# The fold of the attention projections on ScalarE in place of VectorE, and 32 batches in groups of 4, 3 and 1

## What is computed

```python
def _proj(x, W1, b1, W2, b2):
    h = jnp.einsum('bsd,od->bso', x, W1) + b1
    return jnp.einsum('bsd,od->bso', h, W2) + b2
...
qp = _proj(q, W1, b1, W2, b2); kp = _proj(k, W1, b1, W2, b2)
qk = jnp.einsum('bqd,bkd->bqk', qp, kp) * scale + mask
attn = jax.nn.softmax(qk, axis=-1)
return jnp.einsum('bqk,bkd->bqd', attn, v1)
...
x = x + jnp.tanh(g_xattn[0]) * xattn(_layernorm(x), ctx, ctx, mask, W1, b1, W2, b2)
x = x + jnp.tanh(g_ffn[0]) * ffn(_layernorm(x), w1, b1, w2, b2)
```

## Time and profile before

| | us |
|---|---|
| median of 3 runs | 66.02 (65.62 to 68.14) |
| profiled execution | 65.45 |
| its span | 63.7 |
| TensorE busy | 57.5 (90%) |
| VectorE busy | 55.9 (88%) |
| ScalarE busy | 49.5 (78%) |
| GpSimd busy | 43.4 (68%) |

### The profile page before, as it was taken

The page is one execution under the profiler, slowest core; times in us unless marked ns, Lnnn a source line. Parts: engine busy times, 40 slices in busy tenths (PEclk is TensorE's granted clock), DMA queues, the critical chain, the costliest instruction groups (busy, mean ns, idle before and its releaser), DMA issues.

```text
span 63.7 us, 1845 instructions
## 1 busy us (share of the span) xinstructions
PE 57.5 (90%) x541; PEld 44.9 (71%) x541; DVE 55.9 (88%) x313; ACT 49.5 (78%) x137; POOL 43.4 (68%) x88
## 2 busy tenths in 40 slices
PE   4999699899989999989999999999999989998820
PEld 4989447568768775879579699959798849465410
DVE  4659979999999999999999999988999898989630
ACT  2701365597999699999999999999999988867700
POOL 5957599969996805999982996798963948570000
PEclk9999999999999999999999999999999999999998
DMA  0899999999991000000030001330000413041232
GB/s 0 235 395 383 399 416 406 418 408 415 398 396 63 9 0 5 0 5 10 5 124 0 0 0 55 111 140 33 0 0 0 162 42 140 0 165 68 102 124 82
DMA packets 3324, 9.09 MB, mean 143 GB/s; under 512 B 369, under 2 KB 754, under 8 KB 3314
## 3 DMA queue, kind: packets, MB, share of 16 engines
q1 hardware_dynamic: 3312, 8.98, 36.7%
q10 hardware_dynamic: 2, 0.00, 0.0%
HBM read 6.88 MB, written 2.10 MB: 141 GB/s over the span
## 4 chain that ended last, share of the span: by engine, by line
PE 56%; DVE 21%; ACT 5%; DMA 5%; POOL 4%; issue 4%; ACTq 1%; DVEq 0%; POOLq 0%
PE bank_O L545 10%; PE bank_A L504 9%; PE bank_H L530 8%; PE bank_S L488 7%; PE bank_T L464 6%; DVE st L653 6%; PE bank_T L479 5%; DMA load_sb<-in_packed 5%; PE bank_A L497 4%; DVE sc L708 4%; DVE load_sb L720 3%; ACT h L636 3%; POOL rs L381 3%; PE bank_O L540 2%; DVE mv L656 2%
## 5 line engine op out<-in xcount | busy, mean ns | idle before, releaser
L636 ACT ACTIVATE h<-bank_H,fb_q 128x512 int8<-128x512 f32 (+2 forms) x29 | 17.7, 650 | 1.9 <-PE bank_H L530 1.9
L381 POOL TENSOR_TENSOR rs<-ve,half 128x3 f32<-128x3 f32 (+5 forms) x9 | 10.5, 1164 | 8.8 <-DVE nm L661 8.8
L653 DVE BATCH_NORM_STATS2 st<-load_sb 128x6 f32<-128x128 f32 x64 | 14.0, 277 | 1.2 <-DMA load_sb<-in_packed 1.1
L398 POOL TENSOR_SCALAR xq<-load_sb,nm,rs 128x128 int8<-128x128 f32 x28 | 12.4, 459 | 0.9 <-POOL rs L381 0.2
L609 ACT ACTIVATE pr<-sc,mn 128x120 f32<-128x120 f32 x32 | 12.3, 394 | 0.0
L388 POOL TENSOR_SCALAR xn<-load_sb,nm,rs 128x128 f32<-128x128 f32 x22 | 9.7, 451 | 0.5
L504 PE MATMUL bank_A<-load_sb,prT 120*128 120x128 f32 x64 | 9.2, 285 | 0.4 <-ACT prT L618 0.4
L545 PE MATMUL bank_O<-w_q,h 128*128 128x128 bf16 x128 | 9.3, 219 | 0.3
L720 DVE SCALAR_TENSOR_TENSOR load_sb<-bank_A,rec,load_sb 128x128 f32<-128x128 f32 x32 | 9.1, 343 | 0.4 <-issue 0.2
L504 PEld LDWEIGHTS bank_A<-load_sb,prT 120*128 120x128 f32 x64 | 7.8, 191 | 1.9 <-ACT prT L618 1.8
L488 PEld LDWEIGHTS bank_S<-kpT,xaT 128*128 128x128 f32 x64 | 8.1, 191 | 1.3 <-issue 0.8
(11 more groups left out here) (80 smaller groups left out, 96.0 us busy)
## 6 DMA issues: line engine op xcount, KB each, us to landing
load_sb<-in_packed SPq DMA_DIRECT2D x6, 496.0 KB, 8.0
out_y<-y_sb SPq DMA_DIRECT2D x6, 256.0 KB, 2.1
load_sb<-in_packed SPq DMA_DIRECT2D x2, 512.0 KB, 11.1
load_sb<-in_packed SPq DMA_DIRECT2D x1, 576.0 KB, 13.9
load_sb<-in_packed SPq DMA_DIRECT2D x1, 514.0 KB, 6.8
...
```

What stands on the lines that cost most here:

```text
L381: nc.gpsimd.tensor_tensor(rs[:, at], ve[:, at], half[:, 0:at.stop - at.start], ALU.pow).then_inc(rs2_done, 1)
L398: nc.gpsimd.tensor_scalar(low_byte(xq16[g % RING], tile(j)), x_of(g, j), nm2[:, of(g, j, 1)], rs[:, roots(2, g, j)], ALU.add, ALU.mult).th ...
L636: nc.scalar.activation(low_byte(h16[g % RING], hcols(c, g)), bank_H[c][:, cols(g)], ACT.Relu, bias=fb1_q[:, c:c + 1]).then_inc(h_act[c], 1)
L653: nc.vector.bn_stats(st[:, START[g] + j, :], x_of(g, j)).then_inc(st_done, 1)
```

## The change

The six steps of `fold_cp1` and `fold_cp2` are now ScalarE activations, with the same waits. Group 0 has four tiles where it had three, the last group one where it had two. One tile of normalising and one of quantising go from GpSimd to VectorE, and the tile that ScalarE normalises is of group 1 instead of group 0. `DUE` and `FILLERS` have new numbers throughout.

```diff
-TILES = [3, 4, 4, 4, 4, 4, 4, 3, 2]
+TILES = [4, 4, 4, 4, 4, 4, 4, 3, 1]
...
-XN_ON_POOL = [1, 2, 3, 2, 4, 3, 2, 3, 2]
-XN_ON_ACT = [1, 0, 0, 0, 0, 0, 0, 0, 0]
-XQ_ON_POOL = [1, 3, 4, 4, 4, 4, 4, 3, 1]
+XN_ON_POOL = [1, 2, 3, 2, 4, 3, 2, 3, 1]
+XN_ON_ACT = [0, 1, 0, 0, 0, 0, 0, 0, 0]
+XQ_ON_POOL = [1, 3, 3, 4, 4, 4, 4, 3, 1]
...
 DUE = dict(
-    stats1=[380, 574, 771, 1149, 1307, 1670, 2499, 3091, 3649],
+    stats1=[385, 517, 727, 1155, 1287, 1834, 2617, 3438, 4074],
...
-FILLERS = [9, 28, 2, 2, 5]
+FILLERS = [10, 22, 14]
...
+            def fold_cp1():
...
+                act.wait_ge(fold_mm, 1)
+                nc.scalar.activation(Wc[:, :], bank_H[1][:, 0:D], ACT.Identity, accum_out=Wc_sum[:, :]).then_inc(fold_cp, 1)
+                nc.scalar.activation(bc[:, :], bank_H[1][:, D:D + 1], ACT.Identity, bias=b2_sb).then_inc(fold_cp, 1)
+                act.wait_ge(fold_cp, 2)
+                nc.scalar.activation(lift[:, :], Wc_sum[:, :], ACT.Identity, scale=-1.0, bias=bc[:, :]).then_inc(fold_cp, 1)
+                act.wait_ge(fold_cp, 3)
+                nc.scalar.activation(Wc2[:, :], Wc[:, :], ACT.Identity, scale=float(D), bias=lift[:, :]).then_inc(fold_cp, 1)
+
+            def fold_cp2():
+                act.wait_ge(fold_mm, 2)
+                nc.scalar.mul(Mk[:, :], bank_H[2][:, 0:D], SM_SCALE / D).then_inc(fold_cp, 1)
+                act.wait_ge(fold_mm, 3)
+                nc.scalar.mul(wk_neg[:, :], bank_H[1][:, 2 * D:2 * D + 1], -SM_SCALE / D).then_inc(fold_cp, 1)
...
-            def fold_cp1():
...
-                dve.wait_ge(fold_mm, 1)
-                nc.vector.tensor_scalar(Wc[:, :], bank_H[1][:, 0:D], 1.0, 0.0, ALU.mult, ALU.add,
-                                        accum_out=Wc_sum[:, :]).then_inc(fold_cp, 1)
-                nc.vector.tensor_tensor(bc[:, :], bank_H[1][:, D:D + 1], b2_sb, ALU.add).then_inc(fold_cp, 1)
-                dve.wait_ge(fold_cp, 2)
-                nc.vector.tensor_tensor(lift[:, :], bc[:, :], Wc_sum[:, :], ALU.subtract).then_inc(fold_cp, 1)
-                dve.wait_ge(fold_cp, 3)
-                nc.vector.tensor_scalar(Wc2[:, :], Wc[:, :], float(D), lift[:, 0:1], ALU.mult, ALU.add).then_inc(fold_cp, 1)
```

More of the change, by code:

```diff
@@ new lines @@
+    stats1=[385, 517, 727, 1155, 1287, 1834, 2617, 3438, 4074],
+    fold_mm1=[391],
+    spread_gates=[415],
+    fold_cp1=[434],
+    rstd1=[530, 685, 882, 1300, 1433],
+    negate_mask=[546],
+    fold_mm2=[569],
+    fold_cp2=[612],
+    normalise_pool=[642, 796, 993, 1554, 1650, 2590, 3235, 3725, 4291],
+    normalise_dve=[650, 869, 1129, 1512, 0, 2591, 3547],
+    transpose_x=[698, 1032, 1379, 1745, 2059, 2749, 3612, 4235, 4722],
+    project_keys=[760, 849, 1167, 1566, 1880, 2441, 3264, 3947, 4408],
@@ new lines @@
+    copy_xT=[779, 1097, 1455, 1810, 2190, 2941, 3738, 4297, 4768],
+    copy_keys=[862, 955, 1295, 1668, 1982, 2590, 3366, 4046, 4515],
+    scale_means=[0, 862],
+    scale_weights=[915],
+    normalise_act=[0, 916],
+    scores=[939, 1252, 1652, 2242, 2666, 3046, 3864, 4433, 4881],
+    gate=[1009],
+    row_maxima=[1048, 1428, 1966, 2397, 2921, 3187, 3992, 4540, 5108],
+    widen_weights=[1122],
+    exponentials=[1144, 1503, 2036, 2436, 3039, 3537, 4093, 4602, 5147],
+    transpose_probs=[1333, 1791, 2193, 2618, 3218, 3726, 4272, 4735, 5294],
@@ new lines @@
+    copy_probsT=[1398, 1873, 2258, 2703, 3307, 3930, 4337, 4789, 5418],
+    reciprocals=[1420, 2048, 2253, 2910, 3429, 3981, 4259, 4805, 5519],
+    fold_base=[1428],
+    attend=[1477, 1963, 2352, 2795, 3386, 4010, 4496, 4942, 5529],
+    residual=[1585, 2070, 2486, 3010, 3603, 4149, 4608, 5028, 5618],
+    stats2=[1702, 2262, 2778, 3297, 3776, 4337, 4813, 5128, 5658],
+    rstd2=[1847, 2408, 2923, 3558, 4154, 4516, 4959, 5252, 5739],
+    copy_base=[1857],
+    copy_ident=[1930],
+    split_base=[1958],
@@ new lines @@
+    quantise_dve=[2176, 2752, 3271],
+    quantise_pool=[2193, 2719, 3096, 3864, 4344, 4637, 5080, 5357, 5814],
+    transpose_xq=[2328, 2904, 3475, 4098, 4585, 4917, 5269, 5561, 5870],
+    copy_xqT=[2371, 2989, 3688, 4247, 4717, 5076, 5368, 5660, 5897],
+    hidden=[2527, 3127, 3770, 4317, 4788, 5146, 5438, 5725, 5959],
+    relu1=[2644, 3421, 3987, 4396, 4897, 5249, 5541, 5812, 6014],
+    relu3=[2760, 3478, 0, 0, 4957],
+    relu0=[2825, 3190, 3813, 4456, 4838, 5190, 5482, 5763, 5986],
+    relu2=[2882, 3247, 3870, 4542, 5016, 5309, 5601, 0, 6042],
@@ L111 @@
+    mlp_out=[2929, 3497, 4121, 4607, 5007, 5321, 5578, 5875, 6052],
+    result=[3121, 3712, 4273, 4740, 5237, 5455, 5746, 5981, 6122],
+    relu_dve3=[0, 0, 3916, 4472, 0, 5304, 5548, 5866, 6035],
+    relu_dve2=[0, 0, 0, 0, 0, 0, 0, 5813],
+    keep_warm0=[390.5],
+    keep_warm1=[568.5],
+    keep_warm2=[697.5],
 )
-FILLERS = [9, 28, 2, 2, 5]
+FILLERS = [10, 22, 14]
 class Share(list):
@@ L638, in relu @@
                 return stage
-            schedule(once=dict(copy_ident=copy_ident, gate=gate, negate_mask=negate_mask,
+            schedule(once=dict(fold_cp1=fold_cp1, fold_cp2=fold_cp2, copy_ident=copy_ident, gate=gate, negate_mask=negate_mask,
                                copy_base=copy_base),
@@ L766, in scale_weights @@
                 nc.vector.tensor_scalar(w1_q[:, :], mp_8[:, 0:C * P], 1.0 / W_SCALE, None, ALU.mult).then_inc(w1_up, 1)
-            schedule(once=dict(fold_cp1=fold_cp1, fold_cp2=fold_cp2, scale_weights=scale_weights),
+            schedule(once=dict(scale_weights=scale_weights),
                      stats1=stats1, scale_means=(scale_means, XN_ACT), normalise_dve=(normalise_dve, XN_DVE), row_maxima=row_maxima,
```

## The result

| | us |
|---|---|
| changed kernel, median of 4 executions | 67.12 (66.91 to 67.22) |
| kernel before, median of 4 beside it | 67.06 (65.62 to 68.14) |
| ratio | 1.0194, 95% interval 1.0124 to 1.0264 |
| profiled execution of the changed kernel | 67.22, span 65.4 |

The two medians agree and the ratio doesn't, because both kernels have executions of two kinds, some 1.7 to 2 us apart, and the ratio compares only the quicker kind of the kernel before (65.62 and 66.02) with the four of the changed kernel, which are all of the slower kind. The forecast was 65.7 us and no change within 2%, with a range of 64.7 to 67.0.

The account below looks back on a forecast made before the run. Bound by an opening of loads and waits, a TensorE middle with two other engines almost as full, and a tail; terms -0.05 + 0.31 + 0.2 - 0.75 = -0.3 us, from 66.02 to 65.7 us, range 64.7 to 67.0.

Parts of the forecast that it names:

- the four terms: Opening -0.05 us, work moved in or out of the middle +0.31, new gaps in the middle +0.2, tail -0.75.
- the pricing of the opening: Start up to hidden(0): one tile more done, hidden(0) 0.88 us later; -0.05 us, ends -0.4 and +0.5.
- The fold on ScalarE: Start: the chain to Wc2 takes 1.33 us against 0.88 on VectorE; Mk ready at about 7.05; costs nothing.
- a cover of 0.9 us: Start: Mk is ready about 0.9 us before project_keys(0), which waits behind transpose_x(0) for the last normalised tile.
- Rival C: Start: the fold decides, Mk comes last and scores(0) slips; 66.4 us, chance 0.10.
- the 4.01 of my count: Start: the first transfer grows by 128 columns, +0.18 us, so statistics of group 0 run from 4.01.
- my wait of 0.24 us: Opening: VectorE, free at about 5.34, waits until 5.58 for x of group 1.
- term 2: Middle: one tile's MLP moves in from the tail, +0.55 us, and the last attend, 0.24, goes out; +0.31.
- +0.2 with an end of +0.8: Middle: new TensorE gaps, transpose_probs(2) waiting about 0.5 us, partly got back later; +0.2 us, ends -0.2 and +0.8.
- rival A: Middle: late row_maxima(2) isn't got back, TensorE idles at transpose_probs of groups 2, 3 and 4; 67.2 us, chance 0.15.
- The tail: From hidden(6) on: last group halves, relus, matmuls, result and store shrink, one attend comes in; -0.75 us, ends -1.0 and -0.4.

Follow-up runs that it names:

- c1_after_again: The changed kernel unaltered, run again: six executions from 65.51 to 67.54 us, the profiled one 65.51.
- c2: The changed kernel with no short matmuls (0 in place of 10) ahead of the first load: four executions at 66.99 to 68.37 us, ratio 1.0162.
- d3: The changed kernel with 40 small short matmuls in place of 10 in the first row: median 66.66 us, the profiled one 68.29.
- f2: The changed kernel with 18 small short matmuls in place of 10 in the first row, measured once more: median 66.54 us, six of twelve at 67.2 to 67.8.
- f4: The changed kernel with one short matmul in all in place of 90: 67.19 us, executions at 66.45 to 67.85.
- c3_maxima_first: The changed kernel with 18 short matmuls in the first row and row_maxima(2) ahead of stats1(5) on VectorE: 66.00 us median of 12.
- e1_bridge_gap: The changed kernel with 18 short matmuls in place of 10 ahead of the first wait: 66.23 us median of 10, ratio 0.9962.
- d1: The changed kernel with short matmuls of twice the size in each direction and half as many: median 65.65 us, 4 of 12 late.
- e2: The kernel before without its first nine short matmuls: 66.11 us median of 10, ratio 0.9956.
- e4: The kernel before with the fold's six steps on ScalarE, nothing else changed: 67.15 us median of ten, ratio 0.9982.

## Why the prediction was wrong

**The likely time came, but not in the executions that were measured first, and in part by luck.** An early execution of the changed kernel takes 65.3 to 65.9 us (ten of 22) against the forecast of 65.7. By medians it is 0.5 to 0.6 us quicker than an early one of the kernel before, where I had said 0.3. But the traces show no gain: 65.51 in `c1_after_again` against 65.45 for the trace that I added my terms to, which should have given 65.15. The 0.57 us from the profiled execution to the median, which I carried over, hid this miss; why early executions of the kernel before lie anywhere from 65.0 to 67.0 isn't shown. The first four executions were late ones, at 67.1, and give the ratio of 1.0194. One sum of the prediction is wrong besides: the low ends of the four terms add up to 64.7 us, not 64.3.

**The step that failed** is the pricing of the opening: I took every TensorE piece there at the speed that one trace of the kernel before showed (matmuls of 0.038 us, transposes at 0.11 a tile), and had no term and no rival for a TensorE that is still slow. "Followed through its waits, `hidden(0)` starts near 25.85" is what `c1_after_again` shows, 25.84; in the trace of the late execution it is 27.58 (both read at the weight loads of its later chunks), 1.74 later. From there on the two traces take the same time to `hidden(6)`, 28.9 us, and the same to the last `result`, 7.0. I had two hints: the times of the kernel before, 65.62, 66.02 and 68.14, are two kinds, and I read them as scatter; and the first matmuls of that trace, 53 of them in 3.04 us, stood beside 28 in 1.07.

The Trainium skill ("TensorE: Matmul & The Clock Gate", Part 1) says that the point at which matmuls speed up moves from run to run for the same kernel, and the traces agree. It also says that the ramp costs less than 1% of a typical kernel's span; here a late one costs 1.41 us of 65.5 more than an early one, 2.2%, since it lies on a chain of dependent steps and sets when every engine gets its first work. The measurement decides.

**The fold on ScalarE: its length right, its cover wrong.** From the start of `Wc` to the end of `Wc2` it took 1.28 us (4.89 to 6.17 in `c1_after_again`) against 1.33, `Mk` was ready at 7.03 against 7.05, and the transposes and not `Mk` held keys 0 back. But I wrote that the fold costs nothing, under a cover of 0.9 us, since the transposes wait for normalising. The chain of `c1_after_again` says otherwise:

```profile
5.77 0.41 ACT Wc L577
...
6.22 0.49 PE bank_H L439 x2
6.71 0.12 PE bank_H L440 x2
6.83 0.56 PE bank_H L428 x14
7.38 0.59 PE bank_T L477 x4
7.97 0.81 PE bank_H L462 x2
```

The fold, `fold_mm2` and the row of 14 short matmuls lead to the transposes, which stand behind them on TensorE. I had looked only at who waits for `Mk`, and gave those 14 (0.56 us, and 0.88 in the late trace) no term. The cover along this path is small: the last normalised tile of VectorE is ready at 7.55, and the transposes have begun by then. Taking away only this row was not tested. Moving the fold back to VectorE cost 0.86 us in the one pair of early traces, since it stands ahead of normalising there. The Trainium skill ("ScalarE: Activation LUTs", Rules for kernel authors) says to use VectorE, not ScalarE, for adds and multiplies; that pair of traces goes against it. Rival C didn't happen in the early executions. In the late one `Mk` came at 8.04, and the row of 14 short matmuls still held the transposes back, not it.

**The load: right in sign, wrong in place.** The first load came at 3.82 to 4.04 in the early traces (3.64 to 3.83 before), near the 4.01 of my count. In the late first trace it came at 4.33, but in the other late ones of the changed order (`c2`, `d3`, `f2`, `f4`) at 3.86 to 3.92, so a late load isn't what makes them late. VectorE didn't wait for x of group 1 or for the MLP's weights: in `c1_after_again` it found these there at 9.17, where I had them landing at 9.96, so my wait of 0.24 us for the first and the one for the second are not in the traces. `row_maxima(0)` starts at 10.90 against 11.05 all the same, but bounded by `scores(0)` and not by the weights' load.

**The middle: the term was too small.** From `hidden(0)` to `hidden(6)` the kernel before took 29.03 us, and by my terms 0.64 us of work went (0.95 into the opening, less the 0.31 of term 2). The early executions of the changed kernel take 28.9, so 0.5 us of new waits, where I had +0.2 with an end of +0.8. My sign for rival A came too: TensorE is busy 35.65 of the 38 us from 16 to 54 in `c1_after_again` and 36.01 in the first trace, less than 36.8. But its price, 1.5 us more than the forecast, didn't. `row_maxima(2)` starts at 20.30, as I said, but `c3_maxima_first` shows that it costs nothing. In the early traces the chain goes over VectorE from about 31.3 to 37.8, where `transpose_probs(5)` waits for `residual(4)` and the statistics ahead of it; I didn't test that place.

**The tail: right in size.** From `hidden(6)` to the end of the last `result` it takes 6.96 us in `e1_bridge_gap` (55.00 to 61.96), against 6.9 forecast and 7.5 before. I had priced relus and copies and hardly thought of the last group's own way: its `attend` now stands behind `hidden(6)`, and TensorE waits for its quantising, as `c1_after_again` shows:

```profile
58.99 0.22 PE L517 MATMUL bank_H<-ident_h,xq 128*128 128x128 bf16 x1 [0.61 <-POOL xq L396]
```

The last store of 64 KB lands in 1.5 us, 0.2 under the one of 128 KB; I had 0.15.

**What stays open.** That full-size short matmuls in an unbroken row make late executions rarer is shown by counts (0 of 12 against 6 of 12 beside it, and 14 of 34 in all). Size alone left 4 of 12 in `d1`, as many as the unaltered kernel had beside it. The longer row of small ones in `d3` left 1 of 12, which counts can't tell from 0, so that size is needed isn't shown; nor is it in the kernel before (1 of 24 against 11 of 64 beside it). Why an execution of one and the same program turns out one way or the other isn't shown. An idle time of 0.2 us did no harm in the trace of `e2`, and none at all didn't help in `e4`, `d3` and `f2`. I haven't shown either whether the changed kernel's share of late executions (12 of 22) against the other's (21 of 110) comes from the later load, from the fold on ScalarE (five of ten in `e4`, with the order and the load of before) or from what TensorE does after it.
